# Sixteen-head attention: score banks as a pair and a single, and two query tiles per head with their maximum as a + relu(b - a)

## The reference, cut to what matters

```python
norm = 1.0 / np.sqrt(KEY_DIM)          # KEY_DIM = 128 // 16 = 8
Q = jnp.einsum('bsd,hdk->hbsk', q, W_query)
K = jnp.einsum('bsd,hdk->hbsk', q, W_key)
V = jnp.einsum('bsd,hdv->hbsv', q, W_val)
scores = norm * jnp.einsum('hbqk,hbnk->hbqn', Q, K)
attn = jax.nn.softmax(scores, axis=-1)
heads = jnp.einsum('hbqn,hbnv->hbqv', attn, V)
out = jnp.einsum('hbqv,hve->bqe', heads, W_out)
```

## Time and profile before

| | us |
|---|---|
| median of 3 runs | 1708.72 (1704.78 to 1709.45) |
| the profiled execution, its own time | 1715.36 |
| its span, first to last instruction | 1713.6 |

### The profile page before, as it was taken

One profiled execution on the slowest core, in us unless ns is written; L12 is line 12 of the kernel. 1 busy time (PEld: TensorE's weight loads), 2 busy tenths in 40 slices (PEclk: granted clock), 3 DMA queues, 4 the chain that ended last, 5 costly groups with the idle time before them and its releaser, 6 DMA issues. The chain is left out here.

```text
span 1713.6 us, 29866 instructions
## 1 busy us (share of the span) xinstructions
PE 1235.2 (72%) x10684; PEld 622.0 (36%) x10684; DVE 1288.4 (75%) x3515; ACT 907.1 (53%) x1773; POOL 238.4 (14%) x277
## 2 busy tenths in 40 slices
PE   7899999999999996575993533060316999924676
PEld 4122222222222223455972432030114556623345
DVE  6999999999999943355347237989797468578783
ACT  5699999999999995332510212030003575612463
POOL 3000000000000000013310333030004221000223
PEclk9899999999999998667995676565657788965668
DMA  2100001000000000010004431000001811031000
GB/s 73 39 21 21 20 24 28 27 23 21 21 22 25 16 2 16 1 29 1 1 1 188 122 74 37 0 0 0 1 0 51 217 53 46 5 116 50 22 22 31
DMA packets 45030, 62.88 MB, mean 37 GB/s; under 512 B 12785, under 2 KB 34356, under 8 KB 44484
## 3 DMA queue, kind: packets, MB, share of 16 engines
q1 hardware_dynamic: 38243, 49.71, 9.7%
q0 software_dynamic: 5440, 10.67, 2.5%
q10 hardware_dynamic: 1200, 0.59, 0.1%
HBM read 34.10 MB, written 13.63 MB: 28 GB/s over the span
## 5 line engine op out<-in xcount | busy, mean ns | idle before, releaser
L939 DVE TENSOR_REDUCE l0att_half_negmax<-l0att_ps_m 128x1 f32<-128x1024 f32 x480 | 547.2, 1215 | 6.0 <-PE l0att_ps_m L747 6.0
L879 ACT ACTIVATE l0att_probs<-l0att_ps_sv 128x512 f32<-128x512 f32 x960 | 521.2, 596 | 45.3 <-PE l0att_ps_sv L841 33.4
L779 PE MATMUL l0att_ps_sv<-l0att_probs,l_V_aug 128*32 128x256 f32 x4096 | 325.7, 392 | 4.8 <-ACT l0att_pv_sb L863 4.7
L841 PE MATMUL l0att_ps_sv<-l_Q,l_K 51*128 51x512 bf16 x992 | 194.8, 389 | 4.0 <-ACT l0att_probs L887 2.4
L747 PE MATMUL l0att_ps_m<-l_K,l_Q 48*128 48x512 bf16 x960 | 186.2, 385 | 9.3 <-DVE l0att_half_negmax L939 7.1
L779 PEld LDWEIGHTS l0att_ps_sv<-l0att_probs,l_V_aug 128*32 128x32 f32 x4096 | 83.3, 108 | 197.2 <-issue 100.8
L841 PEld LDWEIGHTS l0att_ps_sv<-l_Q,l_K 51*128 51x128 bf16 x992 | 48.1, 93 | 207.5 <-ACT l0att_probs L879 188.1
L472 POOL CAST l0att_nm<-l0att_negmax 128x16 bf16<-128x16 f32 x16 | 3.1, 196 | 497.2 <-DVE l0att_negmax L902 497.2
L2922 ACT ACTIVATE l3loc_probs<-l3loc_ps_s 128x320 f32<-128x320 f32 x128 | 48.9, 435 | 36.5 <-PE l3loc_ps_s L2899 35.9
L2100 DVE SCALAR_TENSOR_TENSOR l2spk_lif_v<-l2spk_U 128x64 f32<-128x64 f32 (+1 forms) x368 | 61.7, 212 | 0.0
L2365 PE MATMUL l2spk_ps<-l_X,l2spk_w_terms 128*128 128x512 bf16 x48 | 13.4, 451 | 61.2 <-DVE l_X L2395 61.2
(11 more groups left out here) (758 smaller groups left out, 2397.8 us busy)
## 6 DMA issues: line engine op xcount, KB each, us to landing
l_K<-l_kp SPq DMA_DIRECT2D x192, 32.0 KB
l_Q<-l_qp SPq DMA_DIRECT2D x192, 32.0 KB
l1ffn_W<-in_l_expert_w_dram SPq DMA_DIRECT2D x1, 4096.0 KB
l3f_experts_l_w<-in_l_w_dram SPq DMA_DIRECT2D x2, 2048.0 KB
l_sorted_in<-l1ffn_zeros SPq DMA_DIRECT2D x1, 3072.0 KB
l1exp_rows<-l_sorted_in SPq DMA_DIRECT2D x6, 512.0 KB, 5.5
l_sorted_out<-l1exp_y SPq DMA_DIRECT2D x6, 512.0 KB, 4.6
l_Q<-in_local_mask_q_dram POOLq DMA_DIRECT2D x2, 1170.0 KB, 20.5
```

The costliest lines, as they stand in the source:

```text
L779: mm = pe.matmul(ps_v[32 * c:32 * c + 32, cols], V_aug[:, kt, h, :], probs[:, kt % 2, c, cols], start=(kt == 0 and part == 0), stop=(kt == ...
L841: pe.matmul(dst, K[at, h % HEAD_BUFS, c1(kt)], Q[at, h % HEAD_BUFS, c4(2 * pair + i)], start=True, stop=True).then_inc(last_scored[i] if l ...
L879: act.activation(probs[:, kt % 2, c, :], ps_s[:, n % 3, :], ACT.Exp).then_inc(expd, 1)
L939: dve.tensor_reduce(half_negmax[:, h % 2, t, half:half + 1], src, AX_X, ALU.max, negate=True).then_inc(m_read, 1)
```

## The change

Four things change in `stage_l0_attend`, for heads 1 to 15 (maxima) and 0 to 14 (scores).

- The ring of ScalarE is no longer three banks of one unit each but a pair (banks 0 and 1) and a single (bank 2), used in turn. A turn of the ring is an "op": even ops take two units in one 1024-wide exp, odd ones one unit. TensorE may write op j when op j - 2 is done (`act_done`). `probs` becomes a ring of 13 slots.
- For query tiles 8 and 12 of each head the maximum is made as in head 0: a pair turn of the ring (an "above" op) holds b - a, made by four products (`difference`), ScalarE takes its relu, and two to three ops later a turn "low" of `ps_m` holds a; one fused pass of VectorE takes the place of two reductions. GpSimd makes the negated rows of these two tiles in `Q_both`.
- The order is planned anew: `attend_turns` lists the uses of `ps_m`, `attend_plan` spreads them evenly over the ops, and puts at most one value group behind each op (`fill`).
- Products with 48 or 51 rows take the two halves of the array's rows alternately through the whole order (`rows_of`), since singles make the count odd.

```diff
+def attend_turns():
+
+    turns = []
+    for head in range(1, L0_H):
+        for t in range(NT):
+            if t == 1 and head == 1:
+                turns.append(("nm", 0))
+            if t in ABOVE_TILES:
+                turns.append(("low", head, t))
+                continue
+            for half in range(2):
+                if t == 1 and half == 1 and head > 1:
+                    turns.append(("nm", head - 1))
+                turns.append(("max", head, t, half))
+    return turns + [("nm", L0_H - 1), ("pv", L0_H - 2), ("pv", L0_H - 1)]
+
+
...
+def attend_plan(turns):
+
+    ahead = turns.index(("max", 1, LEAD, 0))
+    heads = turns.index(("nm", L0_H - 1))
+    units = (L0_H - 1) * NT * NC4
+    count = 2 * (units + 2 * (L0_H - 1) * len(ABOVE_TILES)) // 3
+    slot_of = [(i - ahead) * count // heads for i in range(len(turns))]
...
+    for j in range(count):
+        if j in above_at:
+            ops.append(("above", *above_at[j]))
+            continue
+        size = 1 if j % 2 else min(2, units - n)
+        ops.append(("exp", n, size))
+        op_of += [j] * size
+        n += size
+    assert n == units and len(above_at) == (L0_H - 1) * len(ABOVE_TILES)
...
+        at = slot_of[i] + (4 if i == heads else 0)
+        if i >= ahead and at < count and what[0] != "pv":
+            fill[at].append(what)
+    waiting, group = [], 0
+    for j in range(count):
+        while group < units // NC4 and op_of[NC4 * group + NC4 - 1] + 2 <= j:
+            waiting += [("value", group, part) for part in range(2)]
+            group += 1
+        if waiting:
+            fill[j].append(waiting.pop(0))
+    waiting += [("value", left, part) for left in range(group, units // NC4) for part in range(2)]
+    return ahead, ops, op_of, fill, waiting
+
...
+                    if h + 1 < L0_H:
+                        pool.wait_ge(nm_ready, h + 1)
+                        pool.wait_ge(loaded[(h + 1) % HEAD_BUFS], LOAD * (h // HEAD_BUFS + 1))
+                        for half in range(2):
+                            rows = slice(HALF_ROWS * half, HALF_ROWS * half + TERMS)
+                            pool.tensor_scalar(above_tiles(Q_both[rows, :]),
+                                               above_tiles(Q[rows, (h + 1) % HEAD_BUFS, :]), -1.0, None,
+                                               ALU.mult).then_inc(negated, 1)
...
+                def rows_of(terms):
+                    nonlocal side
+                    at = slice(HALF_ROWS * side, HALF_ROWS * side + terms)
+                    side = 1 - side
+                    return at
...
+                    unit = (h * NT + kt) * NC4
+                    if part == 0 and h < L0_H - 1:
+                        pe.wait_ge(act_done, op_of[unit + NC4 - 1] + 1)
...
-                for h in range(L0_H):
-                    pe.wait_ge(nm_placed[h % 2], 2 * 16 * (h // 2 + 1))
-                    for kt in range(NT):
-                        todo = list(plan[h, kt])
...
-                            elif n >= 2:
-                                pe.wait_ge(expd, n - 1)
-                            for i in range(2):
-                                at = slice(HALF_ROWS * i, HALF_ROWS * i + WITH_MAX)
-                                dst = last_pair[pair][:, i * BANK:(i + 1) * BANK] if last else ps_s[:, (n + i) % 3, :]
-                                pe.matmul(dst, K[at, h % HEAD_BUFS, c1(kt)],
-                                          Q[at, h % HEAD_BUFS, c4(2 * pair + i)], start=True,
-                                          stop=True).then_inc(last_scored[i] if last else scored[i], 1)
...
+                def score(n, bank):
+                    h, kt, c = n // (NT * NC4), n // NC4 % NT, n % NC4
+                    if n % (NT * NC4) == 0:
+                        pe.wait_ge(nm_placed[h % 2], 2 * 16 * (h // 2 + 1))
+                    at = rows_of(WITH_MAX)
+                    return pe.matmul(ps_s[:, bank, :], K[at, h % HEAD_BUFS, c1(kt)], Q[at, h % HEAD_BUFS, c4(c)],
+                                     start=True, stop=True)
+
+                def difference(h, t):
+                    if t == ABOVE_TILES[0]:
+                        pe.wait_ge(negated, 2 * h)
+                    for q, keys in ((Q[:, h % HEAD_BUFS, :], 2), (Q_both, 0)):
+                        for i in range(2):
+                            at = rows_of(TERMS)
+                            mm = pe.matmul(ps_s[:, i, :], q[at, c1(t)], K[at, h % HEAD_BUFS, c4(keys + i)],
+                                           start=(keys == 2), stop=(keys == 0))
+                            if keys == 0:
+                                mm.then_inc(pair_scored[i], 1)
+
+                for j, what in enumerate(ops):
+                    if j >= 2:
+                        pe.wait_ge(act_done, j - 1)
+                    if what[0] == "above":
+                        difference(*what[1:])
+                    elif j % 2:
+                        score(what[1], 2).then_inc(single_scored, 1)
+                    else:
+                        for i in range(2):
+                            score(what[1] + i, i).then_inc(pair_scored[i], 1)
+                    for filler in fill[j]:
+                        if filler[0] == "value":
+                            values(filler[1] // NT, filler[1] % NT, filler[2])
+                        else:
+                            run(filler)
...
-                for n in range((L0_H - 1) * NT * NC4):
-                    kt, c = n // NC4 % NT, n % NC4
-                    if n >= NT * NC4 and kt == 1 and c == 0:
-                        copy_values(n // (NT * NC4) - 1)
-                    act.wait_ge(scored[n % 2], n // 2 + 1)
-                    if n // NC4 >= 2:
-                        act.wait_ge(pv_done, n // NC4 - 1)
-                    act.activation(probs[:, kt % 2, c, :], ps_s[:, n % 3, :], ACT.Exp).then_inc(expd, 1)
...
+                for j, what in enumerate(ops):
+                    if j - 4 in last_op:
+                        copy_values(last_op[j - 4])
+                    if what[0] == "above":
+                        u = above_ops.index(j)
+                        for done in pair_scored:
+                            act.wait_ge(done, j // 2 + 1)
+                        if u >= 3:
+                            act.wait_ge(m_read, place["low", *ops[above_ops[u - 3]][1:]] + 1)
+                        act.activation(above[:, u % 3, :], ps_pair, ACT.Relu).then_inc(act_done, 1)
+                        continue
+                    _, n, size = what
+                    held = held_by[exp_ops.index(j)]
+                    if held >= 0:
+                        act.wait_ge(pv_done, held + 1)
+                    at = prob_at[n]
+                    if j % 2:
+                        act.wait_ge(single_scored, j // 2 + 1)
+                        act.activation(probs[:, at, :], ps_s[:, 2, :], ACT.Exp).then_inc(act_done, 1)
+                    else:
+                        for done in pair_scored:
+                            act.wait_ge(done, j // 2 + 1)
+                        act.activation(probs[:, at:at + 2, :].rearrange("p c n -> p (c n)"), ps_pair,
+                                       ACT.Exp).then_inc(act_done, 1)
...
+                    elif what[0] == "low":
+                        u = lows.index(what)
+                        dve.wait_ge(act_done, above_ops[u] + 1)
+                        dve.tensor_tensor_reduce(above[:, u % 3, :], src, above[:, u % 3, :], -1.0, -LOWEST, ALU.add,
+                                                 ALU.min, half_negmax[:, h % 2, what[2], 0:1]).then_inc(m_read, 1)
```

More of the change, by code:

```diff
@@ new lines, in prob_slots @@
+def prob_slots(sizes):
+    first, before, holder, at, n = [], [], [-1] * PROB_SLOTS, 0, 0
+    for size in sizes:
+        at = 0 if at + size > PROB_SLOTS else at
+        before.append(max(holder[at:at + size]))
+        for i in range(size):
+            first.append(at + i)
+            holder[at + i] = (n + i) // NC4
+        at, n = at + size, n + size
+    return first, before
+def stage_l0_attend(nc, loads, g, V_aug, qp, kp, Q, K, ones_placed, loaded_first, Q_both, K_both, O):
+    turns = attend_turns()
+    place = {what: i for i, what in enumerate(turns)}
+    negate_before = {place["max", h + 1, 0, 0] if h + 1 < L0_H else place["nm", h]: h for h in range(L0_H)}
+    ahead, ops, op_of, fill, waiting = attend_plan(turns)
+    above_ops = [j for j, what in enumerate(ops) if what[0] == "above"]
+    exp_ops = [j for j, what in enumerate(ops) if what[0] == "exp"]
+    prob_at, held_by = prob_slots([ops[j][2] for j in exp_ops] + [2] * (2 * NT))
@@ L740, in run @@
                     dst = ps_m[:, n % 2, :]
[L741 to L742 removed]
+                    if what[0] in ("max", "low"):
+                        _, h, t, half = what if what[0] == "max" else (*what, 0)
                         if t == 0 and half == 0:
@@ L853, in _ @@
                 for part in range(2):
```

(7 more changed lines are left out.)

127 lines of the change are left out of this document (65 added, 62 removed).

## The result

The changed kernel takes 1804.58 us (median of 4 runs, 1802.61 to 1806.66) against 1709.09 for the kernel before beside it: a ratio of 1.0529, 95% interval 1.0487 to 1.0571. The forecast was slower, 1775 us with 1735 to 1800 around it; the sign is right and the time lies 5 us beyond the upper end. Scaled by the ratio to the 1708.7 from which the forecast started, the change comes out at 1799, just inside. Either way it is 24 to 30 us above the middle of the forecast, at the edge of what rival 2 was given (1800 to 1815).

The account below looks back on a forecast made before the run. VectorE was taken to set the head, TensorE 0.3 us behind. TensorE's 586 us plus ring waits gave 627 against 560.9, +66: 1708.7 + 66 = 1775 us, forecast 1755 to 1795 (chance 0.60), range 1735 to 1800.

Parts of the forecast that it names:

- rival 2: Layer 0 attention: clumped maxima hold TensorE's next score, 0.1 us in each of 340 rounds, 1800 to 1815 us; chance 0.10.
- VectorE's gain is on offer only if nothing else is slower than 35.1: VectorE's work per head falls 2.25 us to 35.1, 33.7 us over 15 heads, if no other engine is slower.
- Rival 4: TensorE's cycle is held by ScalarE, so VectorE's 35.1 us sets the head: 1675 us; chance 0.05.
- TensorE stands 0.3 us behind VectorE: Kernel before: TensorE needs 37.0 us of a 37.33 us head that VectorE sets, so 0.3 us of air.
- A lone product costs a place of 0.225, a value group 0.658: TensorE's prices: an unpaired half-array product costs 0.225 us like a bf16 pair, a value group with tile changes 0.658.
- Rival 3: Lone products on TensorE ride for free: head 37.0 us against 37.33, -4 us, 1704, no tellable difference; chance 0.05.
- The floor of 586 (+5): TensorE's own work, 39.1 us a head, 586 in 15 heads, plus 5 for waits behind pv_sb: +30 us.
- Rival 1: Floor only: waits for the ring come to little, 590 us, +30, about 1735 to 1750 us; chance 0.20.
- The ring as a loop: TensorE's scores wait for ScalarE's exp before last: 1.50 to 1.59 us a round at least, 34 to 47 us of waiting.
- The waits behind pv_sb and the start: TensorE's waits behind pv_sb, 5 us in the floor, fall partly into the ring's waits; none added to the forecast.
- The rest of the program as before: Outside the changed heads nothing moves: head 0 and the last head stay as before.
- The sum: 15 heads take 627 us against 560.9, +66: profiled 1715.4 + 66 = 1781, as a median 1775 us.

## Why the prediction was right, and where it was too small

- **VectorE's gain is on offer only if nothing else is slower than 35.1.** Right. Its work fell, and the fall became waiting for TensorE. Rival 4 (TensorE's cycle held by ScalarE) falls with the half reductions in the kernel before and with the short exp, where full rounds don't move by 0.01 us.
- **TensorE stands 0.3 us behind VectorE.** Right in kind: 36.77 measured for 37.0.
- **A lone product costs a place of 0.225, a value group 0.658.** Right: 0.21 in the kernel before; and the rounds with 4 places and 2 groups take 2.214, which is 4 x 0.225 + 2 x 0.657. Rival 3 falls. The Trainium skill says in "TensorE: Matmul & The Clock Gate", section "Packing small matmuls — row/col tiling", that products on different row groups overlap. Rows agree with it for one pair (356.07, both lines), but there the second maxima product comes a place later, its group ending 0.59 behind its start instead of 0.38: an odd count of products spoils the pairing of the ones that follow.
- **The floor of 586 (+5).** No kernel ran at the floor alone. For it speak the prices just named, to which full rounds keep, and that with the loop cut to 1.19 the stretch still is 610.5 where the same sum gives 598. Rival 1, that the waits for the ring come to little, falls: the short exp gives 35 us back.
- **The ring as a loop, 1.50 to 1.59 us, 620 to 633 in sum, 627 taken.** Here lies the largest error. The mechanism held round by round; its size did not. The loop is 1.618 (0.54 + 1.02 + 0.055), and with it the same sum over the same 340 rounds gives 638. Both ends were too low. The upper one rests on the 0.51 of the last head, where I took ScalarE to wait for two semaphores, "as each pair turn now does". The code has three in both places: `last_scored` twice and `pv_done` there, `pair_scored` twice and `pv_done` here. So their number can't make the 0.03 between 0.51 and 0.54. What differs is where they stand. An exp waits for one semaphore itself, and a waiting instruction in front of it takes the others:

```profile
L886 ACTq EVENT_SEMAPHORE  x32: 146/352/847, 626.5 to 656.4; - x32
...
L878 ACTq EVENT_SEMAPHORE  x952: 17/17/17, 72.0 to 625.9; - x191
...
L1008 ACTq EVENT_SEMAPHORE  x242: 38/38/38, 140.8 to 639.6; - x121
...
L1006 ACTq EVENT_SEMAPHORE  x242: 17/17/17, 140.7 to 636.7; - x121
```

  (Lines of the kernel before, last head and ring; of the changed kernel's pairs; of the pairs with one semaphore. In ns, shortest, median and longest.) In the last head this instruction waits for `pv_done` and one score and ends 0.46 behind the scores' start; in the changed kernel's pairs it waits for both scores, is 38 ns long and ends at 0.49; with one semaphore for the pair it is 17 ns long and ends at 0.47. The exp starts 0.045 later in all three. Where the exp's only wait is the pair's it starts at 0.46. And in the ring of the kernel before, each exp waits for two, yet starts 0.42 behind its product where ScalarE was idle, since `pv_done` came early and its wait lay in cover. That this order of the waits is the reason for the 0.03 is read from the traces; no run changed it alone. The lower end, 1.50, was for a single wait, which no pair turn has and which gave 1.536 where it was tried. I took a middle between the two.
- **The waits behind pv_sb and the start, taken at nothing.** 645.3 - 638 = 7 us remain. The first four rounds take 12.0 us (65.14 to 77.11) where their work and the loop give 7.4, so some 4.5 of the 7 lie there. Two things are late:

```profile
65.14 0.63 PE L909 MATMUL l0att_ps_sv<-l_Q,l_K 51*128 51x512 bf16 x2
...
65.88 1.28 ACT L1009 ACT_TABLE_LOAD   x1 [11.95 <-PE l0att_ps_sv L909]
...
71.03 1.08 PE L860 MATMUL l0att_ps_sv<-l0att_probs,l_V_aug 128*32 128x256 f32 x8
```

  TensorE's records are 0.6 and 1.08 long there, with a granted clock of 0.50 (the level of 1.2 GHz) up to 76.5 us and 1.00 behind it; TensorE was busy 4.5 of the 10 us ahead of the first score, and without a gap from 71 us until the clock rose. And ScalarE's table for exp is loaded only when the first score is there, since the load stands behind the instruction that waits for both scores. With one semaphore for the pair it was loaded at 53.19, long before, and the first round took 2.26 us instead of 3.12. The other 2 to 3 us, pv_sb among them, were not divided.
- **The rest of the program as before.** It measured 4.2 us more (1091.4 to 1087.2). Between 1082.0 and 1093.3 in the other kernels, with the same instructions, it is scatter of single executions.
- **The sum.** 66 forecast for the stretch, 84.2 measured: 11 from the loop's size, 7 from what I took at nothing. With the 4 behind it that is the 88.2 us between the two spans.

## What to carry to other kernels

When a buffer ring is made coarser, work out its loop (producer to consumer, the consumer's instruction, the signal back), and take the first part from a place where the consumer waits for the same semaphores in the same order, read in the code and not guessed; then compare it with the producer's work round by round, since what a light round waits is not given back by a heavy one. Relief for the busiest engine is worth only the distance to the next one: here 0.6 us in 37.3, while the price was paid on that next engine. And an odd number of half-array products costs like the next even one.

## What the runs showed of the hardware

- The start of a pair's exp behind its scores depends on which waits end last and where they stand. In the ring: 0.54 us with two semaphores for the scores and `pv_done`, 0.52 with one and `pv_done`, 0.46 with one alone, seen as loops of 1.618, 1.596 and 1.536 us. Their number alone doesn't give it: 0.51 with three in the last head, and 0.42 with two, one of them long done, in the kernel before.
- A table load of ScalarE stands behind the instruction that waits for several semaphores, and ahead of a wait that the exp makes itself: 65.88 us (11.95 idle before it) against 53.19 with one semaphore for the pair and 54.10 in the kernel before.
- Two value groups in a row cost less than two apart: a score pair, a maxima pair, a single and two groups take 1.755 us, where 3 x 0.225 + 2 x 0.657 = 1.99 holds for groups apart. The second of two groups thus costs about 0.42 instead of 0.66, so part of a value group's price is the change between half-array bf16 and full-height fp32 products, paid once for both.
- GpSimd's two negations took 1.76 us a head (48x256 each) and stayed hidden: it still waited 1.44 us for the maxima's copy at 403.67, against 3.83 before.
